# Stage one of an attention and expert layer: x transposed in one run, logits and values transposed behind one query product

## The reference, cut to what matters

```python
xn = layernorm(x)                                   # x: 4 x 2048 x 512, float32
q, k, v = xn @ Wq, xn @ Wk, xn @ Wv                 # 16 heads on 4 key heads, width 32
attn = softmax(mask(q @ k.T * scale)) @ v           # causal
logits = xn @ gate_w.T                              # 32 experts in 8 groups; 3 groups kept, 6 experts chosen
slot = expert * 96 + position_among_the_choices     # choices past 96 for an expert are dropped
moe = sum over the 6 choices of 16 * prob * expert(xn)
shared = (silu(xn @ Wsg) * (xn @ Wsu)) @ Ws_down    # inner width 704
out = x + attn @ Wo + moe + shared
```

## Time and profile before

| | us |
|---|---|
| median of 3 runs (lowest, highest) | 3503.53 (3503.22, 3506.6) |
| the profiled execution's own time | 3499.38 |
| its span | 3497.6 |
| stage one within it | 0 to about 1112 |
| a chunk of the loop | 67.29 |

### The profile page before, as it was taken

How to read it: one execution, slowest core, us unless ns; L and a number is a source line. 1 busy time by engine, 2 the same in 40 slices (tenths; PEclk the granted TensorE clock), 3 DMA queues, 4 the chain that set the end, 5 groups by cost and what they waited for, 6 DMA issues and landing times. The chain is left out here.

```text
span 3497.6 us, 57376 instructions
## 1 busy us (share of the span) xinstructions
PE 3449.9 (99%) x19864; PEld 2227.8 (64%) x19864; DVE 2167.2 (62%) x5314; ACT 1604.8 (46%) x3331; POOL 2071.4 (59%) x1598
## 2 busy tenths in 40 slices
PE   7999999999998999999999999999999999999999
PEld 5888888888886555555555555555555555555487
DVE  6455454555543333777777777777777777777344
ACT  3232232222221111666666666666666566666611
POOL 0332342332334232887978887897889788878800
PEclk9999999999999999999999999999999999999999
DMA  5333223333326997232022202221220222030186
GB/s 183 102 110 113 85 101 119 100 105 114 105 90 187 315 309 229 57 68 65 26 66 69 62 24 71 63 52 37 68 63 26 68 68 62 24 80 29 36 316 235
DMA packets 259882, 358.68 MB, mean 103 GB/s; under 512 B 89628, under 2 KB 99356, under 8 KB 259672
## 3 DMA queue, kind: packets, MB, share of 16 engines
q1 hardware_dynamic: 232936, 326.36, 31.2%
q0 software_dynamic: 17920, 12.82, 1.8%
q10 hardware_dynamic: 8816, 16.82, 1.3%
HBM read 234.16 MB, written 121.38 MB: 102 GB/s over the span
## 5 line engine op out<-in xcount | busy, mean ns | idle before, releaser
L1531 ACT ACTIVATE prb<-banks 128x512 f32<-128x512 f32 (+3 forms) x2560 | 1158.3, 557 | 638.2 <-PE banks L1628 632.7
L1555 DVE TENSOR_REDUCE mx<-banks 128x1 f32<-128x512 f32 x1496 | 957.8, 681 | 333.4 <-PE banks L1613 333.4
L400 POOL DMA_INDIRECT tab_s<-pay,slot x384 | 378.4, 985 | 726.2 <-DVE tokf L691 484.1
L1473 POOL TENSOR_TENSOR rows<-rows,prb 128x1024 f32<-128x1024 f32 x252 | 596.9, 2394 | 0.0
L1558 DVE CUSTOM_DVE_ANT_0 banks<-banks,bias 128x384 f32<-128x384 f32 x981 | 499.0, 525 | 116.8 <-PE banks L1613 114.8
L1640 PE MATMUL ops<-prb,vst 128*32 128x512 f32 (+3 forms) x5120 | 557.2, 534 | 3.3 <-POOL prb L1454 3.2
L1628 PE MATMUL banks<-w_hi,x_hi 97*128 97x512 f32 (+2 forms) x1280 | 494.4, 396 | 3.2 <-DVE ones_b L1548 1.7
L1628 PE MATMUL banks<-w_lo,x_lo 97*128 97x512 f32 (+2 forms) x1280 | 484.6, 396 | 1.2 <-ACT prb L1531 0.5
L1613 PE MATMUL banks<-x_lo,w_lo 96*128 96x512 f32 (+2 forms) x1280 | 463.5, 375 | 0.0
L1613 PE MATMUL banks<-x_hi,w_hi 96*128 96x512 f32 (+2 forms) x1197 | 436.7, 377 | 0.0
L754 PE MATMUL acc<-x_hi,w_hi 128*128 128x512 f32 x1088 | 430.0, 395 | 2.3 <-DVE qk_lo L593 2.1
(11 more groups left out here) (174 smaller groups left out, 4203.7 us busy)
## 6 DMA issues: line engine op xcount, KB each, us to landing
wgu<-in_e_gu SPq DMA_DIRECT2D x24, 1408.0 KB, 7.0
rows<-in_x SPq DMA_DIRECT2D x16, 1024.0 KB, 7.7
xn_s<-rows SPq DMA_DIRECT2D x16, 1024.0 KB, 5.1
y_sb<-in_x SPq DMA_DIRECT2D x16, 1024.0 KB, 5.3
q_hi_s<-qk_hi SPq DMA_DIRECT2D x16, 1024.0 KB, 4.2
q_lo_s<-qk_lo SPq DMA_DIRECT2D x16, 1024.0 KB, 6.5
base<-y_sb SPq DMA_DIRECT2D x16, 1024.0 KB, 4.3
w_hi<-q_hi_s SPq DMA_DIRECT2D x64, 256.0 KB, 5.9
```

The lines of the kernel that those rows point to most:

```text
L400: nc.gpsimd.indirect_dma_start(t["tab"], bass.IndirectOffsetOnAxis(ap=slot[:, i, k:k + 1], axis=0), pay[:, i, k, :], None, bounds_check=E ...
L1473: nc.gpsimd.tensor_tensor(acc4, acc4, prb[:, slot(bg, n, pr)], ALU.add).then_inc(add_done, 1)
L1531: nc.scalar.activation(prb[:, slot(bg, k, h // 2), h % 2, q0:CH], bank("score", bg, GROUP * k + h)[:, q0:CH], ACT.Exp, scale=SCALE).then_i ...
L1555: V.tensor_reduce(mx[:, h * NKT + qt, j:j + 1], held[:, 0:wr], AX.X, ALU.max).then_inc(mred_done, 1)
```

## The change

The next chunk's x is transposed in one run of 16 behind y0. Its four slices go into four banks: the two of `xtp`, `smp`, and the third bank of `acc`. TensorE no longer waits between slices; it waits ahead of them until `lt` and the positions of the current chunk have been read. VectorE takes all four low parts behind the addition of y0. `lt` and `vt` both go behind i = 2, the first query product, in the 15 chunks of the loop; `lt` goes into a bank of `xtp` in every chunk. In VectorE's list `low(4)` and `glu(0)` stand ahead of the copy of the indices and the marks in these 15 chunks. Chunk 15 keeps its order. In the transposes before the loop (chunk 0) nothing is waited for between slices either.

The diff, without the moved text of `glu` and without the renamed index in the transposes of `vt`:

```diff
@@ stage_a, PSUM buffers
         smp = ps("smp", [P, CH])
+        turned = [xtp[:, 0, :], xtp[:, 1, :], smp[:], acc[:, ACCB - 1, :]]
@@ ScalarE, xhi(c)
-                    nc.scalar.activation(x_hi[:, k, :], xtp[:, k % 2, :], ACT.Copy).then_inc(xhi_done, 1)
+                    nc.scalar.activation(x_hi[:, k, :], turned[k], ACT.Copy).then_inc(xhi_done, 1)
@@ VectorE, xlo(c)
-                    V.tensor_tensor(x_lo[:, k, :], xtp[:, k % 2, :], x_hi[:, k, :].bitcast(F32),
+                    V.tensor_tensor(x_lo[:, k, :], turned[k], x_hi[:, k, :].bitcast(F32),
                                     ALU.subtract).then_inc(xlo_done, 1)
@@ VectorE, body: the definition of glu(m) stands earlier, unchanged
-                V.tensor_reduce(lg[:], smp[:, 0:2 * NT * E].rearrange("p (t h e) -> p t e h", h=2, e=E), AX.X,
+                V.tensor_reduce(lg[:], xtp[:, 0, 0:2 * NT * E].rearrange("p (t h e) -> p t e h", h=2, e=E), AX.X,
                                 ALU.add).then_inc(lt_read, 1)
...
                 low(3)
+                if nxt:
+                    low(4)
+                    glu(0)
                 link(V.tensor_copy(i8f[:], i8[:]), c)
...
-                low(4)
                 if not nxt:
+                    low(4)
                     positions()
                     entries()
-                glu(0)
+                    glu(0)
...
-                if nxt:
-                    xlo(c + 1, (0, 1))
                 dve.wait_ge(xr_in, c * 16 + 16)
                 for i in range(NT):
-                    if nxt and i == 2:
-                        xlo(c + 1, (2, 3))
+                    if nxt and i == 1:
+                        xlo(c + 1)
                     dve.wait_ge(y_done, c * NT + i + 1)
@@ TensorE
-            def transposes(c, ks=range(KC)):
+            def transposes(c):
 
                 pe.wait_ge(ln_done, c * NT + NT)
-                for k in ks:
-                    if not isinstance(c, int) or c * KC + k >= 2:
-                        pe.wait_ge(xlo_done, c * KC + k - 1)
+                if not isinstance(c, int) or c:
+                    pe.wait_ge(lt_read, c)
+                    pe.wait_ge(pos_read, 2 * c)
+                for k in range(KC):
                     for i in range(NT):
-                        last = nc.tensor.transpose(xtp[:, k % 2, i * P:(i + 1) * P],
+                        last = nc.tensor.transpose(turned[k][:, i * P:(i + 1) * P],
                                                    xn[:, i, k * P:(k + 1) * P], ident[:])
                     last.then_inc(xt_done, 1)
...
-                    if i == 1:
+                    if i == (2 if nxt else 1):
                         pe.wait_ge(l_done, c + 1)
-                        pe.wait_ge(pos_read, 2 * c)
                         pe.sem_inc(pe_pass, 1)
-                        for i in range(NT):
-                            last = nc.tensor.transpose(smp[:, 2 * i * E:2 * (i + 1) * E], l_f[:, i * P:(i + 1) * P],
+                        for n in range(NT):
+                            last = nc.tensor.transpose(xtp[:, 0, 2 * n * E:2 * (n + 1) * E], l_f[:, n * P:(n + 1) * P],
                                                        ident[0:2 * E, 0:2 * E])
                         last.then_inc(lt_psum, 1)
-                    elif i == 3:
+                    if i == (2 if nxt else 3):
                         pe.wait_ge(v_done, c + 1)
-                        pe.wait_ge(lt_read, c + 1)
...
-                if nxt:
-                    transposes(c + 1, (0, 1))
                 pe.wait_ge(w_lo_done, NPC)
                 pe.wait_ge(hlo_done, c * FM + FM - 1)
                 for i in range(NT):
-                    if nxt and i == 2:
-                        transposes(c + 1, (2, 3))
+                    if nxt and i == 1:
+                        transposes(c + 1)
                     pe.wait_ge(ysb_done, c * NT + i + 1)
```

More of the change, by code:

```diff
@@ L594, in low, with glu @@
                                     ALU.subtract).then_inc(qlo_done, 1)
+                def glu(m):
+                    last = m == FM - 1
+                    rows = FT if last else P
+                    i = FIRST_F + 2 * m
+                    if last:
+                        dve.wait_ge(acc_done, c * NACC + i + 1)
+                        V.tensor_copy(up_t[:], acc[FT:2 * FT, i % ACCB, :]).then_inc(upt_done, 1)
+                        dve.wait_ge(upt_done, c + 1)
+                        up = up_t[:]
+                    else:
+                        dve.wait_ge(acc_done, c * NACC + i + 2)
+                        up = acc[:, (i + 1) % ACCB, :]
+                    dve.wait_ge(sil_done, c * FM + m + 1)
+                    dve.wait_ge(hlo_done, c * FM + m)
+                    V.tensor_tensor(h_sb[0:rows, :], sil[0:rows, :], up, ALU.mult).then_inc(glu_done, 1)
+                    dve.wait_ge(hhi_done, c * FM + m + 1)
+                    low_rows = h_hi[FT:2 * FT, m, :] if last else h_lo[:, m, :]
+                    V.tensor_tensor(low_rows, h_sb[0:rows, :], h_hi[0:rows, m, :].bitcast(F32),
+                                    ALU.subtract).then_inc(hlo_done, 1)
                 dve.wait_ge(lt_psum, c + 1)
-                V.tensor_reduce(lg[:], smp[:, 0:2 * NT * E].rearrange("p (t h e) -> p t e h", h=2, e=E), AX.X,
+                V.tensor_reduce(lg[:], xtp[:, 0, 0:2 * NT * E].rearrange("p (t h e) -> p t e h", h=2, e=E), AX.X,
                                 ALU.add).then_inc(lt_read, 1)
@@ L650, in body @@
                                     ALU.add).then_inc(mask_done, 1)
-                def glu(m):
-                    last = m == FM - 1
-                    rows = FT if last else P
-                    i = FIRST_F + 2 * m
-                    if last:
-                        dve.wait_ge(acc_done, c * NACC + i + 1)
-                        V.tensor_copy(up_t[:], acc[FT:2 * FT, i % ACCB, :]).then_inc(upt_done, 1)
-                        dve.wait_ge(upt_done, c + 1)
-                        up = up_t[:]
-                    else:
-                        dve.wait_ge(acc_done, c * NACC + i + 2)
-                        up = acc[:, (i + 1) % ACCB, :]
-                    dve.wait_ge(sil_done, c * FM + m + 1)
-                    dve.wait_ge(hlo_done, c * FM + m)
-                    V.tensor_tensor(h_sb[0:rows, :], sil[0:rows, :], up, ALU.mult).then_inc(glu_done, 1)
-                    dve.wait_ge(hhi_done, c * FM + m + 1)
-                    low_rows = h_hi[FT:2 * FT, m, :] if last else h_lo[:, m, :]
-                    V.tensor_tensor(low_rows, h_sb[0:rows, :], h_hi[0:rows, m, :].bitcast(F32),
-                                    ALU.subtract).then_inc(hlo_done, 1)
                 def positions():
@@ L792, in body @@
                         product(c, i, col, P)
-                    if i == 1:
+                    if i == (2 if nxt else 1):
                         pe.wait_ge(l_done, c + 1)
-                        pe.wait_ge(pos_read, 2 * c)
                         pe.sem_inc(pe_pass, 1)
-                        for i in range(NT):
-                            last = nc.tensor.transpose(smp[:, 2 * i * E:2 * (i + 1) * E], l_f[:, i * P:(i + 1) * P],
+                        for n in range(NT):
+                            last = nc.tensor.transpose(xtp[:, 0, 2 * n * E:2 * (n + 1) * E], l_f[:, n * P:(n + 1) * P],
                                                        ident[0:2 * E, 0:2 * E])
                         last.then_inc(lt_psum, 1)
-                    elif i == 3:
+                    if i == (2 if nxt else 3):
                         pe.wait_ge(v_done, c + 1)
-                        pe.wait_ge(lt_read, c + 1)
-                        for i in range(NT):
-                            last = nc.tensor.transpose(smp[:, i * P:(i + 1) * P], v_f[:, i * P:(i + 1) * P], ident[:])
+                        for n in range(NT):
+                            last = nc.tensor.transpose(smp[:, n * P:(n + 1) * P], v_f[:, n * P:(n + 1) * P], ident[:])
                         last.then_inc(vt_psum, 1)
```

## The result

The changed kernel takes 3541.88 us (median of 4 runs, 3539.53 to 3543.38), the kernel before 3503.69 on the same chip (3503.22 to 3506.6): a ratio of 1.0108, 95% interval 1.0096 to 1.0120. The forecast was 3501.4. It is 38 us slower and far outside the range.

The account below looks back on a forecast made before the run. TensorE, 99% busy, was taken as the bound. Savings of 1.2 (lt with vt), 0.3 (x run) and 1.8 us (start), less 1.2 lost at y0, gave 2.1: 3503.5 to 3501.4 us, range 3496 to 3507.

Parts of the forecast that it names:

- The adds: VectorE's additions of y and the low parts behind y0, with GpSimd's entries: nothing waits, 0 us.
- Rival 3: In 15 chunks y0 waits on glu(4)'s low part: slower, 3507.0 us, or 3505.5 with the loads; chance 14%.
- lt and vt: Transposes of logits and values put together in 15 chunks: 0.08 us saved a chunk, 1.2 us in all.
- x in one run: Two groups of x transposes become one in each loop chunk: 0.02 us saved a chunk, 0.3 us in all.
- y0 uncovered: y0 directly behind product n = 10, without transposes hiding its entry: 0.08 us lost a chunk, 1.2 us in all.
- The experts' chain: Choice of experts one product later, with VectorE's low parts and marks behind it: nothing waits, 0 us.
- The chunk: Period of one loop chunk: 67.29 us less 0.02.
- The start: Before the loop and in chunk 0: 1.5 us from earlier loads and 0.3 from low(4), 1.8 us saved.
- The gate: TensorE's matmul before chunk 0 that waits for a low part: moves from 23.42 to 21.9 us.
- rival 1: TensorE's low clock behind chunk 0's 2.12 us wait: without it 3500.3 us, with a second one 3502.5; chance 12%.

Follow-up runs that it names:

- i1: The changed kernel with GpSimd's entries started later by two small fills, the run of 16 kept ahead of y1: 3497.05 us, ratio 0.9992.
- g1: The kernel before with its two groups of eight x transposes moved ahead of y1 and y3 instead of y0 and y2: 3531.34 us, ratio 1.0083.
- f4: The changed kernel with the 16 x transposes cut into four groups of four inside y1, entries unmoved: 3497.18 us, ratio 0.9992.
- h2: The changed kernel with four groups of four inside y1 and GpSimd's entries 0.6 us later by two fills: 3495.80 us, ratio 0.9989.

## Why the prediction was wrong

The step that failed is "The adds": "The addition of y1 needs y1, 4 us later, and y3 waits for it a further 4: 0." It takes for granted that a signal leaves when its matmul ends. In the loop y1's signal came up to 5.4 us late, and the addition 2.06 past the time at which y3 could start: 27.0 us of waiting, and 19.1 more for the restarts and the low clock behind them, 46.1 us in the loop instead of 0. The same paragraph said of GpSimd's entries that their conditions "move with TensorE. 0". Their conditions did; but the x row moved from 1.9 us behind their first transfer (414.76 in the trace of before, below; the row at 416.64 in the earlier trace rows) to 5.9 us behind it (429.31 and 435.21), and the prediction never set the row and the transfers side by side. No rival named this. Rival 3 has the right sign and the wrong place: y0 does not wait. Every row of before on time was no evidence that rows beside transfers are safe, only that those rows at those times are.

```profile
414.76 0.97 POOL L400 DMA_INDIRECT tab_s<-pay,slot  x1 [24.83 <-DVE tokf L691]
```

Point by point, the rest held, which the changed kernel shows already and i1, without the late signals, confirms in the total:

- *lt and vt.* Forecast 1.43 us over both. TensorE, answering: 388.69 to 390.13, 1.44.

```profile
388.69 0.39 PE L757 MATMUL acc<-x_hi,w_lo 128*128 128x512 f32 x1
389.01 0.46 PE L800 MATMUL xtp<-ident,l_f 64*128 64x64 f32 x4
389.40 0.66 PE L806 MATMUL smp<-ident,four 128*128 128x128 f32 x4
...
390.13 0.39 PE L757 MATMUL acc<-x_lo,w_hi 128*128 128x512 f32 x1
```

- *x in one run.* From y0's last matmul to y1's second it is 434.98 to 437.19: 2.21, less two steps of 0.233, 1.74. Forecast 16 x 0.105 + 0.04 = 1.72.
- *y0 uncovered.* Product to y0's second matmul:

```profile
430.96 0.39 PE L757 MATMUL acc<-x_hi,w_lo 128*128 128x512 f32 x1
...
431.47 0.40 PE L837 MATMUL yp<-d_hi,h_lo 128*128 128x512 f32 x1
```

  0.51, less 0.227 and 0.233: 0.05, against 0.08. The entry itself, 430.96 to 431.19, is a plain step of 0.23, as the earlier trace rows had it. The rule of the Trainium skill that the prediction names ("TensorE: Matmul & The Clock Gate", Part 3) would by its account have had 0 here; the 0.05 is too small to decide for or against it.
- *The experts' chain.* low(2) ended at 398.64, low(3) at 401.74; with lt at 389.01 for 374.39 of the old count (14.62 on) that is 384.02 and 387.12, forecast 384.0 and 387.5. low(4) waited 2.61 us for ScalarE's copy, to 404.35 (389.7 of the old count), 2.1 later than I had it and still ahead of n = 2 at 391.7: this is the keys' product whose signal was 2.7 late. The marks ended at 397.9, forecast 397.2. Nothing waited: right.
- *The chunk.* 67.29 - 0.02: 67.27 in the one chunk not held, and in i1:

```profile
417.24:484.52 67.28, 67.28 (x320) 54.57 (x319) 34.54 (x84) 18.48 (x29) 24.15 (x26) 1.00 0.31 105
```

  Others of i1 are 67.22; from 148.31 to 1022.38 its 13 periods are 67.24 each.
- *The start.* Gained more than forecast in this trace. TensorE and VectorE, answering, and SyncE's refill, answering:

```profile
15.21 1.94 PE L748 MATMUL xtp<-ident,rows 128*128 128x128 f32 x8 [15.21 <-DVE rows L562]
...
21.66 0.66 PE L781 MATMUL acc<-x_hi,gw 128*64 128x512 f32 x1 [2.80 <-DVE x_lo L568]
...
44.81 0.57 PE L757 MATMUL acc<-x_hi,w_hi 128*128 128x512 f32 x1 [2.41 <-DVE qk_lo L594]
```

```profile
18.93 1.28 DVE L568 TENSOR_TENSOR x_lo<-xtp,x_hi 128x512 fp32r<-128x512 f32 x2
...
39.75 2.47 DVE L532 BATCH_NORM_STATS2 stats<-rows 128x6 f32<-128x512 f32 x4 [2.29 <-DMA rows<-in_x]
```

```profile
22.03 2.14 SPq L340 DMA_DIRECT2D y_sb<-in_w_a  x4
```

  The gate at 21.66 (forecast 21.9), the refill at 22.03, 1.77 earlier. `ln_stats(1)` is at 39.75 (41.0), n = 0 at 44.81 (46.1): 2.8 us gained, not 1.5. But one pair of executions is too little here. Over all traces `ln_stats(1)` starts at 41.2 to 42.7 in the six kernels with the start of before, 42.0 in the mean, and at 39.6 to 41.7 in the thirteen with the changed start and experts' order, 40.5 in the mean. That is 1.6 earlier, and the last product matmul of chunk 0 is 1.9 earlier in the mean (79.4 and 77.5): the forecast had 1.5 and 1.8. The low clock of rival 1 stayed: TensorE was granted 0.50 from 46 to 48 us.

**The sum in hindsight.** Without the held signals it agrees with what was measured: 2.1 us forecast, 3.1 in i1 (3500.11 - 3497.05) and 2.4 without entries (3499.69 - 3497.32), most of it at the start. Both intervals just reach 1, so the size is borne out no closer than that. The failure is in what the sum left out.

## What to carry to other kernels

A signal is a term of its own: where an edit moves a tight row of TensorE operations, or DMA work of GpSimd, set the two side by side in time, and give a consumer that idles behind a finished producer a price. When engines idle although their inputs are complete by the producer's own rows, cut the tight row into fours or move the other stream by some 0.6 us before anything else is tried: both are cheap, and either one removed the whole loss here. After a wait, count the restart and the low clock that follow; here they made 27 us of waiting into 46. And read a gain of a few microseconds at the start off several executions, not off one pair.

## What the runs showed of the hardware that was not expected

- TensorE's completion signals can lag its work: by 1.8 and 3.5 us for slices, up to 5.4 for y1 and some 6.2 in g1, while TensorE itself goes on at full pace, and y1's came 1.8 us after GpSimd's last indirect transfer. ScalarE's and VectorE's signals in the same stretch took 0.03 to 0.05. Rows of four did not bring this about beside the same transfers (f4, h2); rows of eight did. Once it had happened, a plain product beside the next transfers signalled late too, by 2.7.
- GpSimd's indirect transfers come every 1.28 us (0.97 busy, 0.30 between), but one here and there takes 1.07 to 1.54, and a pause of 2.92 to 2.96 appears in a few chunks with nothing named as its cause. In chunk 14 the row behind such a pause was on time.
- A wait of some 2.07 us was followed by a stretch at a granted clock of 0.50, the lower level of 1.2 GHz (matmul starts 0.43 apart), in ten chunks, and not in three with the same wait (periods of 69.7 instead of 71.2).
